# Writing block-diagonal mixing weights on GpSimd from a packed copy, through two buffers

## What is computed

```python
def _spectral_conv(x, w1, w2):
    Bb, _, Hh, Ww = x.shape
    Wf = Ww // 2 + 1
    xf = jnp.fft.rfft2(x).reshape(Bb, G, WID, Hh, Wf)
    ...
    lo = jnp.einsum('bgixy,gioxy->bgoxy', xf[:, :, :, :M1, :M2], w1c)
    hi = jnp.einsum('bgixy,gioxy->bgoxy', xf[:, :, :, Hh - M1:, :M2], w2c)
    ...
    return jnp.fft.irfft2(out_ft.reshape(Bb, G * WID, Hh, Wf), s=(Hh, Ww))
```

## Time and profile before

| | |
|---|---|
| median of three runs | 3073.56 us (3072.54 to 3080.72) |
| the profiled execution | 3098.2 us, its span 3096.2 us |
| busy in the span | PE 2572.4, PEld 1994.0, DVE 1935.2, ACT 1290.9, POOL 1026.9 us |
| moved by DMA | 423.46 MB, of them 381.07 MB in SP's queue |
| HBM | 252.61 MB read, 166.38 MB written |
| mean granted TensorE clock | 0.922 of full speed |

### The profile page before, as it was taken

How to read it: one execution, slowest core, us unless ns; L and a number is a source line. 1 busy time by engine, 2 the same in 40 slices (tenths; PEclk the granted TensorE clock), 3 DMA queues, 4 the chain that set the end, 5 groups by cost and what they waited for, 6 DMA issues and landing times. The chain is left out here.

```text
span 3096.2 us, 46908 instructions
## 1 busy us (share of the span) xinstructions
PE 2572.4 (83%) x18156; PEld 1994.0 (64%) x18156; DVE 1935.2 (63%) x2352; ACT 1290.9 (42%) x2167; POOL 1026.9 (33%) x1050
## 2 busy tenths in 40 slices
PE   0499999685978768999899989898987599999468
PEld 0144444343655457888888878788886488888345
DVE  4988876674852644346565656564754489898633
ACT  1687777463322321233233322233232377766322
POOL 1988810223621400202020101111111377777310
PEclk9999999897989889999998999998988799999789
DMA  8500002567522354589897989897987553551134
GB/s 185 118 0 26 0 26 47 164 182 165 131 54 79 104 100 131 181 215 234 203 240 194 225 198 216 227 215 222 210 215 194 130 98 71 81 102 21 62 99 105
DMA packets 242226, 423.46 MB, mean 137 GB/s; under 512 B 85930, under 2 KB 188970, under 8 KB 217154
## 3 DMA queue, kind: packets, MB, share of 16 engines
q1 hardware_dynamic: 218011, 381.07, 51.4%
q10 hardware_dynamic: 23520, 34.61, 3.8%
q0 software_dynamic: 496, 5.01, 0.4%
HBM read 252.61 MB, written 166.38 MB: 135 GB/s over the span
## 5 line engine op out<-in xcount | busy, mean ns | idle before, releaser
L1589 ACT ACTIVATE fno_act<-fno_pz 128x320 f32<-128x320 f32 x512 | 220.7, 438 | 722.2 <-PE fno_pz L1505 566.6
L1248 DVE STREAM_TRANSPOSE spec_chan<-spec_form_in 128x1024 f32<-128x1024 f32 x256 | 497.6, 1958 | 8.3 <-PEq L238 8.3
L1452 POOL TENSOR_SCALAR fno_xm<-fno_xm 40x384 f32<-40x384 f32 x96 | 114.3, 1190 | 992.4 <-DMA fno_xm<-scratch_modes 992.4
L1505 PE MATMUL fno_pz<-spec_cols,spec_chan 128*128 128x96 f32 x3072 | 395.7, 289 | 8.4 <-issue 8.4
L1505 PEld LDWEIGHTS fno_pz<-spec_cols,spec_chan 128*128 128x128 f32 x3072 | 380.9, 204 | 23.5 <-issue 19.6
L1879 POOL TENSOR_TENSOR head_hact_lo<-head_hact,head_hact_hi 128x512 fp32r<-128x512 f32 x256 | 343.7, 1366 | 136.6 <-DVE head_hact_hi L2021 136.6
L1535 PE MATMUL fno_pw<-fno_fw,fno_act 128*128 128x96 f32 x2560 | 310.9, 281 | 32.6 <-DVE fno_wfreq L1727 25.0
L1535 PEld LDWEIGHTS fno_pw<-fno_fw,fno_act 128*128 128x128 f32 x2560 | 300.6, 196 | 42.0 <-DVE fno_wfreq L1727 32.9
L611 PE MATMUL cml_acc<-cml_logis,cml_mats 128*128 128x512 f32 x480 | 246.8, 596 | 55.9 <-DVE cml_logis L568 55.9
L613 PE MATMUL cml_acc<-cml_moved,cml_mats 128*128 128x512 f32 x480 | 246.2, 594 | 11.2 <-ACT cml_moved L534 11.2
L1717 DVE COPY spec_cols<-fno_pj 48x512 f32<-48x512 f32 (+1 forms) x150 | 88.3, 604 | 222.2 <-PE fno_pj L1515 190.9
(11 more groups left out here) (224 smaller groups left out, 4806.9 us busy)
## 6 DMA issues: line engine op xcount, KB each, us to landing
scratch_form<-fno_act SPq DMA_DIRECT2D x32, 2560.0 KB
spec_form_in<-scratch_form SPq DMA_DIRECT2D x64, 1024.0 KB
fno_wt<-table_mix_w SPq DMA_DIRECT2D x192, 150.0 KB
fno_coef<-scratch_mixed SPq DMA_DIRECT2D x50, 480.0 KB, 9.4
nca_raw<-scratch_xnp SPq DMA_DIRECT2D x66, 329.7 KB
spec_form_in<-scratch_form SPq DMA_DIRECT2D x32, 512.0 KB
scratch_mixed<-fno_om ACTq DMA_DIRECT2D x96, 160.0 KB
scratch_mixed<-spec_om ACTq DMA_DIRECT2D x96, 160.0 KB
```

The costliest lines, as they stand in the source:

```text
L1248: return nc.vector.transpose(chan[:, to * TR * PIX:(to + 1) * TR * PIX].rearrange("p (h q w) -> p h q w", h=TR, q=4), src)
L1505: mm = nc.tensor.matmul(pz[:, t % 4, m * 96:(m + 1) * 96], left, cols[:, h * CS:h * CS + 96] if layer else wz[:, :], start=m == 0, stop=Tr ...
L1589: nc.scalar.activation(act_b[:, :, 4 * t:4 * t + 4], z, ACT.Silu if n >= UNITS else ACT.Copy).then_inc(a_out, 1)
```

## The change

The weights of a layer are laid out packed: per chunk and input channel only the 10 output channels of its own group, 24 x 10 elements, all 12 chunks of a layer in one tensor of 104 rows. SP loads that once per layer, in the unit with n % 8 equal to 3, into `packed`. GpSimd then writes each chunk's full block-diagonal tile into `wt[c % WB]`, WB = 2, by one multiplication: the packed weights, repeated for the four groups, times `own_group`, a table of ones and zeros that says to which group a row belongs. `feed(q)` sets the order of these multiplications (`unpack`) and the turns of the spectra (`turn_modes`) on GpSimd; `begin_mix` becomes the bare `store_modes`, and `feed_mix` loads spectra alone. PE waits for `wt_full` in place of the transfers' semaphores. The blanking of `wt` keeps its line and has two buffers to fill.

```diff
--- before.py
+++ after.py
@@ -195,12 +195,16 @@
     m[SB:128, 0], m[0:CH, 1], m[:, 2] = (np.repeat(betas.T, n, axis=0) for n in (S2 * WID, WID, FC))
     m[64:64 + CH, 1] = m[0:CH, 1]
     c["betas"] = m.reshape(128, 3 * LAYERS)
-    m = z(LAYERS, 2, CHUNKS // 2, 2, G, WID, XC, KY, G, WID)
+    m = z(LAYERS, 2, CHUNKS // 2, 2, G, WID, XC, KY, WID)
     for half, name in enumerate(("L2_conv_sp_w1", "L2_conv_sp_w2")):
         w = inp[name].reshape(LAYERS, G, WID, WID, CHUNKS // 2, XC, KY, 2).transpose(4, 7, 1, 0, 2, 5, 6, 3)
         for g in range(G):
-            m[:, half, :, :, g, :, :, :, g, :] = w[:, :, g].transpose(2, 0, 1, 3, 4, 5, 6)
-    c["mix_w"] = m.reshape(LAYERS, CHUNKS, 2 * CH, XC * KY, CH)
+            m[:, half, :, :, g] = w[:, :, g].transpose(2, 0, 1, 3, 4, 5, 6)
+    m, m2 = m.reshape(LAYERS, CHUNKS, 2, CH, XC * KY * WID), z(LAYERS, MR, CHUNKS, XC * KY * WID)
+    m2[:, 0:CH], m2[:, 64:MR] = m[:, :, 0].transpose(0, 2, 1, 3), m[:, :, 1].transpose(0, 2, 1, 3)
+    c["mix_w"], c["own_group"] = m2, z(MR, G)
+    for g in range(G):
+        c["own_group"][g * WID:(g + 1) * WID, g] = c["own_group"][64 + g * WID:64 + (g + 1) * WID, g] = 1.0
     m, m2 = z(CS, S2, 128), z(128, S2, 16)
     for g in range(G):
         f = slice(FC * g, FC * g + FC)
@@ -1221,7 +1225,7 @@
 
 XC = 2
 CHUNKS = NX // XC
-XB, OB = 5, 6
+XB, OB, WB = 5, 6, 2
 MR = 64 + CH
 PER, MIX_AT = CHUNKS // 2, 3
 FH = B * KY // 2
@@ -1287,7 +1291,8 @@
         wz = ph.sb("wz", [128, 96])
         xm = ph.sb("xm", [128, XB, XC, 2, FH])
         om = (ph.sb("om", [MR, OB // 2, 2, UNITS * ST]), om_kept)
-        wt = ph.sb("wt", [128, XB, XC * KY, CH])
+        wt = ph.sb("wt", [128, WB, XC * KY, CH])
+        packed, own_group = ph.sb("packed", [MR, CHUNKS, XC * KY * WID]), ph.sb("own_group", [MR, G])
         work = ph.sb("work", [128, 6, 3 * LAYERS])
         wbias = ph.sb("wbias", [CH, LAYERS])
         pz = ph.ps("pz", [128, 4, NB])
@@ -1300,7 +1305,8 @@
             ph.sem(n) for n in ("tables", "set_up", "beta_in", "step", "scaled", "fill_pool", "fill_act"))
         (z_done, a_out, turned, act_stored, w_done, c_out, h_done, d_out, both_out, coef_in, j_done, j_out) = (ph.sem(n) for n in (
             "z_done", "a_out", "turned", "act_stored", "w_done", "c_out", "h_done", "d_out", "both_out", "coef_in", "j_done", "j_out"))
-        wt_in, x_in = ([ph.sem(f"{n}{b}") for b in range(XB)] for n in ("wt_in", "x_in"))
+        x_in = [ph.sem(f"x_in{b}") for b in range(XB)]
+        packed_in, own_in, wt_full = ph.sem("packed_in"), ph.sem("own_in"), ph.sem("wt_full")
         x_full, j_out_v = ph.sem("x_full"), ph.sem("j_out_v")
         mix_done, out_v, out_s = ph.sem("mix_done"), ph.sem("out_v"), ph.sem("out_s")
 
@@ -1345,11 +1351,10 @@
                         sp.dma_start(coef[2 * NX * half:2 * NX * (half + 1), :, :],
                                      mixed[:, :, half * 20:half * 20 + 20, at:at + 2 * ST].rearrange("r x c f -> (r x) c f")).then_inc(coef_in, 16)
 
-                def load_weights(c):
-                    if c >= XB:
-                        sp.wait_ge(mix_done, c - XB + 1)
-                    for half in range(2):
-                        sp.dma_start(wt[64 * half:64 * half + CH, c % XB, :, :], k["mix_w"][c // (2 * CHUNKS), c % CHUNKS, CH * half:CH * half + CH]).then_inc(wt_in[c % XB], 16)
+                def load_weights(layer):
+                    if layer:
+                        sp.wait_ge(wt_full, 2 * CHUNKS * layer)
+                    sp.dma_start(packed[:, :, :], k["mix_w"][layer]).then_inc(packed_in, 16)
 
                 def load_modes(c):
                     if c >= XB:
@@ -1365,11 +1370,6 @@
                         sp.dma_start(modes[:, :, i2:CH:2, f].rearrange("k x c f -> (k x) c f"),
                                      both[48 * i2:48 * i2 + 48, :, :, :].rearrange("p c u f -> p c (u f)")).then_inc(both_out, 16)
 
-                def begin_mix(q):
-                    for c in range(XB):
-                        load_weights(q * CHUNKS + c)
-                    store_modes(2 * q + 1)
-
                 def first_modes(q):
                     sp.wait_ge(both_out, 64 * (q + 1))
                     for c in range(XB):
@@ -1378,7 +1378,6 @@
                 def feed_mix(c):
                     if c % CHUNKS + XB < CHUNKS:
                         load_modes(c + XB)
-                        load_weights(c + XB)
 
                 for t in range(S2):
                     for i in range(2):
@@ -1397,6 +1396,7 @@
                 sp.dma_start(form_in[R0 + 2 * C:KX, 1, :], k["coords"]).then_inc(tables, 16)
                 sp.dma_start(fh[:, :, :], k["fh"]).then_inc(tables, 16)
                 sp.dma_start(ih[:, :], k["ih"]).then_inc(tables, 16)
+                sp.dma_start(own_group[:, :], k["own_group"]).then_inc(own_in, 16)
                 sp.wait_ge(set_up, 2)
                 sp.dma_start(wsm[SB:128, :, :], k["point_w"]).then_inc(tables, 16)
 
@@ -1404,8 +1404,10 @@
                     layer, u = n // UNITS, n % UNITS
                     if n == 4:
                         sp.wait_ge(mix_blank, 2)
+                    if n % UNITS == 3:
+                        load_weights(layer)
                     if n % 4 == 0 and n:
-                        begin_mix(n // 4 - 1)
+                        store_modes(n // 2 - 1)
                     if n % 4 == 2:
                         store_modes(n // 2 - 1)
                     for c in mixed_in(n):
@@ -1429,7 +1431,7 @@
                     if n + 2 >= UNITS:
                         old = n + 2 - UNITS
                         load_unit(sp, form_in, old % 2, form[old // UNITS % 2, old % UNITS], unit_in[old % 2])
-                begin_mix(SIDES - 1)
+                store_modes(2 * SIDES - 1)
                 first_modes(SIDES - 1)
                 for c in last_mix:
                     feed_mix(c)
@@ -1452,6 +1454,34 @@
                     nc.gpsimd.tensor_scalar(x[64:64 + CH, :, 0, :], x[0:CH, :, 1, :], -1.0, None, ALU.mult).then_inc(x_full, 1)
                     nc.gpsimd.tensor_copy(x[64:64 + CH, :, 1, :], x[0:CH, :, 0, :]).then_inc(x_full, 1)
 
+                def unpack(c):
+                    if c == 0:
+                        pool.wait_ge(mix_blank, 2)
+                        pool.wait_ge(own_in, 16)
+                    if c % CHUNKS == 0:
+                        pool.wait_ge(packed_in, 16 * (c // (2 * CHUNKS) + 1))
+                    if c >= WB:
+                        pool.wait_ge(mix_done, c - WB + 1)
+                    nc.gpsimd.tensor_tensor(wt[0:MR, c % WB, :, :].rearrange("p y (g o) -> p y g o", g=G),
+                                            wide(packed[:, c % CHUNKS, :].rearrange("p (y o) -> p y o", o=WID), G, 2),
+                                            wide(wide(own_group[:, :], XC * KY, 1), WID, 3), ALU.mult).then_inc(wt_full, 1)
+
+                def feed(q):
+                    todo = range(q * CHUNKS, (q + 1) * CHUNKS)
+                    pool.wait_ge(x_full, 2 * todo[0])
+                    for c in todo[0:WB]:
+                        unpack(c)
+                    pool.wait_ge(wt_full, todo[0] + WB)
+                    for c in todo[0:XB]:
+                        turn_modes(c)
+                    for c in todo:
+                        if c + WB in todo:
+                            pool.wait_ge(x_full, 2 * min(c + XB, todo[-1] + 1))
+                            unpack(c + WB)
+                        if c + XB in todo:
+                            pool.wait_ge(wt_full, c + WB + 1)
+                            turn_modes(c + XB)
+
                 for n in range(ALL):
                     layer, u = n // UNITS, n % UNITS
                     if u == UNITS - 1:
@@ -1460,11 +1490,9 @@
                         pool.wait_ge(set_up, 2)
                         pool.wait_ge(z_done, (n + 1) * NZ)
                         nc.gpsimd.tensor_copy(cols[:, 0:COLS // 2].rearrange("p (h c) -> p h c", c=CS), wide(wsm[:, layer, :], H // 2, 1)).then_inc(fill_pool, 1)
-                    if n % 4 == 1:
-                        for c in range((n // 4 - 1) * CHUNKS if n > 4 else 0, n // 4 * CHUNKS):
-                            turn_modes(c)
-                for c in range((SIDES - 1) * CHUNKS, SIDES * CHUNKS):
-                    turn_modes(c)
+                    if n % 4 == 1 and n > 4:
+                        feed(n // 4 - 1)
+                feed(SIDES - 1)
 
             @block.tensor
             def _(pe):
@@ -1546,7 +1574,7 @@
                         mm.then_inc(h_done, 1)
 
                 def mix(c):
-                    pe.wait_ge(wt_in[c % XB], 32 * (c // XB + 1))
+                    pe.wait_ge(wt_full, c + 1)
                     pe.wait_ge(x_full, 2 * (c + 1))
                     pj_free(("mix", c))
                     if c == 0:
@@ -1554,7 +1582,7 @@
                     rows = xm[:, c % XB, :, :, :].rearrange("p x r (a y b) -> p x r a y b", y=KY, b=B2)
                     for y in range(KY):
```

(2 more changed lines are left out.)

## The result

The changed kernel takes 3162.3 us (median of four runs, 3152.5 to 3176.3), the kernel before 3077.1 (median of four). The ratio is 1.0251, with an interval of 1.0218 to 1.0284. The forecast was 3138: a loss of 65 us, where the two profiled executions, 3098.2 and 3176.3, stand 78.1 apart.

What follows compares the result with a forecast made beforehand. PE sets the pace and what makes it wait, chiefly late spectra, moves the time. Sides 1 to 6 +58, side 0 +4.1, tail +5.2 and blanking -2.4 give +65 us on 3073.6: 3138, range 3068 to 3192.

Steps and rivals of the forecast that it cites:

- 40 us for the first six chunks: Sides 1 to 6, chunks 0 to 5: mix 5 +4.7 us later plus 2 for the clock, +6.7 a side, six times.
- 36 for the second: Sides 1 to 6, chunks 6 to 11: mix 11 +4.0 us later plus 2 for the clock, +6.0 a side, six times.
- took off 18: Sides 1 to 6: 3 us a side given back by stalls falling into the waits and form stores landing earlier.
- the order on GpSimd decides: Write-out 3 stands behind turn 5, write-out 9 behind turn 11, so PE waits for late spectra; +12.7 us a side before give-back.
- rival of slow write-outs: GpSimd's write-outs take 2.9 us, a pair with a turn 4.76; slower still, +107 us, 3181; chance 0.12.
- In the tail: Side 7, with nothing beside it: chunks +9.7 us, weights gone ahead of the modes' store -4.5, together +5.2.
- The memset: VectorE's blanking of wt: 1920 elements instead of 4800, 1.6 us instead of 4.06, -2.4 straight on PE's path.
- I take 3 us by which chunk 5 arrives earlier: SP's queue, first six chunks: without the weight loads chunk 5's spectra arrive 3 us earlier, bounds 0 and 6.
- 2 us for the clock: PE comes out of an idle stretch slow; 2 us added to each mixed unit's six chunks.
- 1 us for chunk 11: SP's queue, second six chunks: without the few weight loads ahead chunk 11 arrives 1 us earlier, bounds 0 and 3.
- The queue as the bound: With 29.5 MB less in the queue spectra land early enough not to hold write-out 3; faster, -40 us, 3034; chance 0.12.
- The draw: Spectra arrive 7 us earlier, mix 5 stays where it was, other costs are paid; within 0.3%, 3075; chance 0.10.

Runs made afterwards that it cites:

- experiment 1: Changed kernel with another order on GpSimd: write-outs 2, 3, 4 before turn 5, then each turn directly before its own write-out; 0.9968 of the kernel before, 3074.7 us.
- experiment 4: Kernel before, all loads kept, no write-outs; from mix 3 of a side PE also waits for spectra two chunks ahead; 1.0173 of the kernel before.
- experiment 3: Kernel before with only the first five chunks' weights loaded and used for all, no new work on GpSimd; 0.9931 of the kernel before.
- Experiments 5 and 6: 5: later spectra loads on ScalarE's queue; 6: form_in behind spectra. On experiment 1's, changed and prior kernels: 1.0005, 1.0309, 1.0005 and 0.9902, 1.0136, 1.0016.
- experiments 6 and 7: 6: first mixed unit's form_in load put behind spectra, in three kernels; 7: experiment 1's order with the next unit's form_in also put off, 0.9871, 3050.0 us.
- experiment 2: Changed kernel with write-outs of one group's columns only, 104x240 instead of 104x960, the other groups' mixing left out; 1.0172 of the kernel before.

## Why the prediction was right, and where its sizes were off

The direction and the mechanism of the first six chunks were right. That the total came within 20 us is in part luck, for the terms missed in both directions: for sides 1 to 6 it added 40 us for the first six chunks, 36 for the second and took off 18; measured were 57.8, 11.6 and, in the other units, 4.7.

**Right: the order on GpSimd decides.** "Behind it in GpSimd's order stands write-out 3, and PE waits for that at mix 3": experiment 1 removes that and the loss with it, experiment 4 adds only that and gets 1.7%.

**Right: the single prices.** A write-out takes 1.79 us (1.8 forecast); its row on the page:

```profile
L1465 POOL TENSOR_TENSOR fno_wt<-fno_packed,fno_own_group 104x960 f32<-104x960 f32 x96 | 173.0, 1811 | 444.7 <-DMA fno_packed<-table_mix_w 256.3
```

The estimate of 2.1 us from the Trainium skill (GPSIMD Engine Reference, "Performance versus the Vector engine") was too high here. The rival of slow write-outs (2.9 us each) falls with the same row. A pair of turn and write-out is 3.58 us (3.66 forecast). In the tail mix 11 comes 37.2 us after mix 0 instead of 27.3 (+9.9, +9.7 forecast), and mix 0 comes 28.3 us after unit 31's store instead of 34.9 (-6.6, -4.5 forecast). The memset:

```profile
1176.25 1.66 DVE L1787 MEMSET fno_wt<- 128x1920 f32 x1 [0.46 <-issue]
```

is 2.4 us shorter as forecast, but PE got only 2.0 of that back as a shorter wait (11.86 against 13.83), and lost about half of it again in the 60 matmuls behind (9.89 against 8.76 us, at a granted clock of 0.69 against 0.78).

**Off: "I take 3 us by which chunk 5 arrives earlier".** Turn 5 came 16.2 us after mix 0 in the mean of sides 1 to 6, before 16.6. The relief was 0.5 us, and in experiment 3, without the weight loads, also 0.5: they were not what the spectra waited for. The prediction knew that form_in stood ahead, but took it for a matter of the queue. Experiments 5 and 6 show it to be the transfer: a queue of its own leaves the loads late, and form_in out of the way brings turn 5 to 3.7 us after mix 0.

**Off: "2 us for the clock".** Mixes 4 and 5 came 5.4 us apart, not 3.66, so at least 3.5 us in side 2 alone. Its own rows had part of this after a much shorter stall: 3.02 us for 16 matmuls and 1.82 for a mix. With both terms set right side 2 comes out: spectra 17.1 + pair 3.6, then two chunks of 5.4: 31.5, which is what mix 5 shows (25.1 + 2 forecast). In the mean mix 5 came 29.5 us after mix 0 (20.1 before, where the prediction went by the 20.4 of side 2): +9.4, nearly the whole +9.6 of the first units.

**Off: "1 us for chunk 11", and a term that was missing.** Turn 11 came 6.5 to 11.0 us after mix 6, so mix 11 at 20.0 in the mean, 2.8 earlier than before, where 4 later was forecast: write-out 9 does stand behind turn 11, but turn 11 was no longer late enough for that to cost what was forecast. But the second units are 1.9 us longer all the same, since mix 6 itself starts 26.6 us after the store ahead of it and not 21.3: +5.3 a side. ScalarE tells of it. After, then before, in side 2, at the end of the sixth chunk's output; the last four stores of the unit are one row after and two before:

```profile
1637.37 4.20 ACTq L1645 DMA_DIRECT2D scratch_mixed<-spec_om  x4
1641.67 1.07 ACT L1625 ACTIVATE spec_cols<-fno_pj 48x512 f32<-48x512 f32 x2 [3.87 <-issue]
```

```profile
1605.76 0.28 ACTq L1617 DMA_DIRECT2D scratch_mixed<-spec_om  x1
1606.08 1.30 ACTq L1617 DMA_DIRECT2D scratch_mixed<-spec_om  x3
1607.48 1.07 ACT L1597 ACTIVATE spec_cols<-fno_pj 48x512 f32<-48x512 f32 x2 [1.12 <-PE fno_pj L1515]
```

These four issues take 4.20 us where they took 1.62 from the first to the end of the last; in sides 1 to 6 they take 3.6 to 5.6 us after and 1.5 to 1.7 before. The copy of the columns stands behind them, and PE behind the copy (3.22 us instead of 0.64, then 24 matmuls in 4.54 us instead of 3.18). These are the 25 us in PE's waits. The same wait is 43.7 us in experiment 1, 51.2 in experiment 3 and 57.8 in experiment 4, but only 23.4 to 27.1 in the four kernels of experiments 6 and 7. It is there without write-outs (3, 4), with all weight loads (4) and without the bad order (1, 3), so it is no part of the mechanism above. That it is low in all four kernels that put form_in off is a hint and no cause shown, for the kernel before has it low (22.1) with form_in early. It also eats most of the relief: in experiment 3 mix 11 comes 7.7 us sooner after mix 6, and mix 6 5.7 us later after its store. What makes the issues slow was not tested and stays open.

**The rivals.** The queue as the bound (faster, 0.12) falls by experiment 3: without the weight loads the gain is 0.7% (24 us), though nothing is added on GpSimd, and turn 5 stays late. The draw (0.10) falls with the missing 7 us of earlier spectra. Side 0 lost 6.7 us more than forecast (+8.4 against +1.7). In its first six chunks mix 5 came 23.8 us after mix 0 instead of 19.0: three mixes follow at 5.4 us and one at 4.5, where before one follows at 5.4 and one at 4.5, with no wait between. No term held that, and no run took it apart. In its second six mix 11 came 22.9 us after mix 6 instead of 15.2, +7.7 where 4.1 was forecast.

By size the loss is: the wait alone +1.7% (experiment 4), the length of the write-outs +0.8% (experiment 2), the lighter queue -0.7% (experiment 3). These add to 1.8, not 2.5; they are not independent, as ScalarE's wait is in each of them, and the intervals of these runs are 0.6 to 1.1 points wide.

## What to carry to other kernels

When work is moved to an engine that works in order, look not at its duration but at what stands ahead of it there: an operation that needs nothing late, queued behind one that waits for a DMA, inherits that wait, and whoever needs the first one inherits it too. Put all that is ready ahead of the wait; here that order was worth 2.8%, the smaller transfer volume 0.7%. And a late small load is to be traced to the large one whose transfer it shares, by moving that one, before queues are changed.

## What the runs showed of the hardware

After a stall of 11 us PE resumed at a granted clock of 0.52 for 15.3 us of nearly unbroken matmuls, with chunks of 5.4 us instead of 3.03: two such chunks are 4.8 us on top of the stall itself. A load of 0.25 MB on ScalarE's queue, beside 2.13 MB on SP's, took 12 us: nothing of it moved in its first 6 us, and most of it only when SP's transfer was nearly through. And the same four issues on ScalarE's queue took 4.20 us in one kernel and 1.62 in the other. The write-outs of 104x960 with both inputs broadcast took 1.79 us, those of 104x240 0.59 us.
